# The seven activation blocks of batch 1 fetched through another engine's queue

## The chip, the cores and the metric

One core of a Trainium2 chip runs the kernel. The metric is the device time of one execution in microseconds (us). Five engines run programs of their own and meet at semaphores: TensorE (PE), VectorE (DVE), ScalarE (ACT), GpSimd (POOL) and SyncE (SP). SP computes nothing here; it issues transfers (DMAs). ACT can issue transfers as well, from its own queue, in the order of its program. The transfers of both queues are carried by the core's 16 DMA engines.

## The reference

```python
x = L0_attn_hidden_states                      # (2, 1024, 512)
x = x + layernorm(attn(layernorm(x)))          # 32 heads of 128, decaying linear attention
x = x + layernorm(ffn(layernorm(x)))           # ternary weights, FF = 1792

# attn(x):
qkv = silu(x @ qkv_w.T)                        # per head q, k, v of 128
# scan over blocks of the sequence, per head:
scores = (q @ k.T) * diag_decay
out = scores @ v + (q * q_decay) @ kv
kv = kv * block_decay + (k * k_decay).T @ v
# then
normed = norm_w * rms_normalised(out)
result = (sigmoid(x @ gate_w.T) * normed) @ out_w.T
```

## The kernel before

The attention part runs over 16 pairs of heads for batch 0 and then 16 pairs for batch 1, one window per pair and batch: windows 0 to 31 (`PAIRS` is 16, `STEPS` is 32). Window `w` projects K, Q, V and the gate G of its pair (kinds `KK, QQ, VV, GG`) and at the same time finishes the attention of window `a = w - 1`.

Each projection is one step of Strassen's scheme in Winograd's form: seven products of weight combinations with seven activation blocks, `B_11, T_2, T_3, B_21, T_1, B_22, T_4`. A product is written (kind, i); `FACTORS` gives its block: 1 uses B_11, 2 B_21, 3 B_22, 4 T_4, 5 T_1, 6 T_2, 7 T_3. Every operand is split in a high and a low float32r part, so a block in `xb` is 128 partitions x 2 x 1024 values, 8 KB a partition, 1 MB. The blocks of batch 0 are made on the chip. Those of batch 1 are made in window 0 and parked in DRAM (`x_blocks`); they have to replace batch 0's in `xb` at the passage from window 15 to window 16. Block `b` may be overwritten once the last product of window 15 that reads it, (G,i), is done; product (K,i) of window 16 waits for its arrival (`xb_in[b]`). PE's order of the G products is 1, 6, 7, 2, 5, 3, 4, and window 16's K products have the order 1, 6, 7, 2, 5, 3, 4 too.

K and V have to be turned into token order. `turn_k` transposes on DVE, and SP writes the result to DRAM and reads it back (`k_write`, `k_read`); V is written first (`v_write`), read back in four parts of 128 KB (`v_read`, `v_tok<-v_blocks`) and then transposed on DVE (`turn_v(w, s, h)`, halves s of the sequence, heads h). `v_read(w, 1)` goes into the same buffer as `v_read(w, 0)` and waits for its two transposes. The buffer then takes the output weights (`out_weights`, `v_tok<-w_out`), which wait for the transposes of the second read.

The order on each engine is the order in which its program is written. On SP, at the end of a window: `v_write` 1 and 0, `v_read` 0, the weights of V for the next window, `v_read` 1, the decay table, then the next window's G weights and the output weights. On DVE, at the end of a window: `turn_v(w,0,0)`, `finish_12` of G, `turn_v(w,0,1)`, an addition, `finish_21` of G, an addition, `turn_v(w,1,0)`, `turn_v(w,1,1)`. On ACT: the activation of V's last block (`activate(w, VV, OUT21)`), then the four sigmoids of G (`OUT11, OUT22, OUT12, OUT21`); OUT12 waits for `finish_12`, OUT21 for `finish_21`. Behind window 15, DVE reduces the largest integer weights to `part_max` (L1546), and POOL makes an all-reduce over the partitions of it (L717) ahead of its work for window 16, whose first steps are the weight sums `ws` (L530 to L538) of V. ACT's `w_hi` (L852) needs those.

In windows 2 to 15 ACT also issues three small loads `check<-w_ints` per window (L915); they are the only transfers on its queue.

## Time and profile before

| | |
|---|---|
| median of 3 runs | 2528.63 us (2528.07 to 2534.14) |
| the profiled execution's time | 2531.22 us |
| its span, first to last instruction | 2529.1 us |
| granted TensorE clock, mean | 0.976 |
| PE busy | 94% |
| POOL busy | 65% |
| DVE busy | 55% |
| ACT busy | 45% |
| SP's queue (q1) | 269.39 MB, 32.2% of the 16 engines' span |
| ACT's queue (q10) | 11.01 MB, 1.4% |
| `xb<-x_blocks`, SP | 7 transfers of 1024 KB, median 8.4 us from issue to landing |

Times within the trace are us from the start of the span. Idle time of an engine that nobody waits for costs nothing; what matters is whose wait ends last. The window of interest is the passage from window 15 to window 16, about 1060 to 1140.

### The profile page before, as it was taken

What the parts mean: (1) busy time and instruction counts of PE and PEld (TensorE: products, weight loads), DVE (VectorE), ACT (ScalarE), POOL (GpSimd) and SP (SyncE); (2) the same over time, 40 slices, a digit from 0 to 9 for tenths busy, and PEclk for the clock granted to TensorE, in tenths of its full rate; (3) what the DMA queues carried; (4) which work ended last, traced back from release to release, by engine and by line L of the source; (5) the groups of instructions that cost most, each with busy time, mean ns of one, the idle gap of its engine ahead of it and who ended that gap; (6) DMA issues with size and microseconds to landing.
All of it is one profiled execution on the core that took longest, in us unless ns stands there. A gap on an engine that the chain in (4) does not pass through costs nothing.

```text
span 2529.1 us, 38203 instructions
## 1 busy us (share of the span) xinstructions
PE 2384.8 (94%) x12256; PEld 2023.9 (80%) x12256; DVE 1396.5 (55%) x2454; ACT 1140.3 (45%) x1666; POOL 1637.1 (65%) x1311
## 2 busy tenths in 40 slices
PE   4799999999999999989999999999999996799996
PEld 3688888888888888878888888888888885577884
DVE  5456566666666666545555555555555555534347
ACT  6544444444444444434444444444444443643333
POOL 4577777777777777656777777777777763344345
PEclk8899999999999999999999999999999998899998
DMA  3633333333333333444333333333333333101001
GB/s 109 212 120 123 124 124 123 123 121 126 124 118 124 122 124 124 144 173 146 113 112 112 112 112 112 112 112 112 112 112 112 112 100 134 59 26 50 25 25 67
DMA packets 145541, 281.09 MB, mean 111 GB/s; under 512 B 20560, under 2 KB 86096, under 8 KB 143184
## 3 DMA queue, kind: packets, MB, share of 16 engines
q1 hardware_dynamic: 139440, 269.39, 32.2%
q10 hardware_dynamic: 6048, 11.01, 1.4%
q8 instruction: 30, 0.49, 0.1%
q14 instruction: 23, 0.19, 0.0%
HBM read 199.60 MB, written 80.74 MB: 111 GB/s over the span
## 4 chain that ended last, share of the span: by engine, by line
PE 55%; POOL 15%; issue 11%; DMA 7%; DVE 5%; ACT 5%; SPq 1%; POOLq 0%; ACTq 0%; DVEq 0%
PE proj L1750 33%; PE yp L1750 10%; PE sc L1816 3%; POOL qd L567 3%; PE sc L1819 3%; PE sc L1793 3%; PE sc L1806 3%; POOL sumsq L579 2%; POOL g_lo L583 2%; DMA v_tok<-v_blocks 2%; POOL h_lo L684 2%; POOL w_lo L552 2%; DMA k_blocks<-pd 2%; DMA k_tok<-k_blocks 1%; DVE stats L1196 1%
## 5 line engine op out<-in xcount | busy, mean ns | idle before, releaser
L1750 PE MATMUL proj<-xb,w_hi 128*128 128x512 f32 x3584 | 1151.8, 403 | 47.1 <-POOL w_lo L545 12.8
L1750 PEld LDWEIGHTS proj<-xb,w_hi 128*128 128x128 f32 x3584 | 653.3, 191 | 177.0 <-POOL w_lo L545 13.6
L1750 PE MATMUL proj<-xb,w_lo 128*128 128x512 f32 x1792 | 705.3, 394 | 0.0
L1750 PEld LDWEIGHTS proj<-xb,w_lo 128*128 128x128 f32 x1792 | 339.3, 189 | 74.7
L552 POOL TENSOR_TENSOR w_lo<-ws,w_hi 128x1024 fp32r<-128x1024 f32 x128 | 307.4, 2401 | 135.5 <-ACT w_hi L852 135.5
L567 POOL TENSOR_TENSOR qd<-q,table 128x512 f32<-128x512 f32 x128 | 164.6, 1298 | 202.2 <-ACT q L892 202.2
L545 POOL TENSOR_TENSOR w_lo<-raw,w_hi 128x768 fp32r<-128x768 f32 x128 | 235.6, 1841 | 15.5 <-ACT w_hi L846 15.3
L558 POOL TENSOR_TENSOR ow_lo<-v_tok,ow_hi 128x1024 fp32r<-128x1024 f32 x32 | 76.4, 2387 | 248.3 <-ACT ow_hi L860 248.3
L1385 DVE TENSOR_TENSOR g<-sc,g 128x512 f32<-128x512 f32 x128 | 88.4, 691 | 241.9 <-ACT sq L906 241.8
L1392 DVE TENSOR_TENSOR y<-yp,y 128x512 f32<-128x512 f32 x240 | 163.6, 682 | 93.7 <-PE yp L1750 93.2
L1750 PE MATMUL yp<-ow_hi,g_hi 128*128 128x512 f32 x512 | 204.8, 400 | 10.4 <-POOL g_lo L583 5.6
L1750 PE MATMUL yp<-ow_hi,g_lo 128*128 128x512 f32 x512 | 201.0, 393 | 0.0
L1750 PE MATMUL yp<-ow_lo,g_hi 128*128 128x512 f32 x512 | 201.0, 393 | 0.0
L1816 PE MATMUL sc<-pd,v 128*128 128x128 f32 x1024 | 188.7, 276 | 9.6 <-DVE state L1377 9.6
L1750 PE MATMUL proj<-x_hi,f_hi 128*128 128x512 f32 x448 | 177.2, 396 | 8.7 <-DVE x_lo L1576 8.6
L684 POOL TENSOR_TENSOR h_lo<-hid,h_hi 128x512 fp32r<-128x512 f32 x56 | 72.3, 1290 | 163.1 <-ACT h_hi L1106 163.1
L1816 PEld LDWEIGHTS sc<-pd,v 128*128 128x128 f32 x1024 | 161.1, 193 | 19.6 <-issue 9.7
L1750 PE MATMUL proj<-x_lo,f_hi 128*128 128x512 f32 x448 | 176.7, 394 | 0.0
L1819 PE MATMUL sc<-qd,state 128*128 128x128 f32 x896 | 174.3, 276 | 0.0
L583 POOL TENSOR_TENSOR g_lo<-g,g_hi 128x512 fp32r<-128x512 f32 x128 | 162.4, 1294 | 8.6 <-ACT g_hi L911 8.6
L1346 DVE STREAM_TRANSPOSE v<-v_tok 128x512 f32<-128x512 f32 x128 | 86.6, 696 | 144.9 <-DMA v_tok<-v_blocks 144.9
L579 POOL TENSOR_TENSOR sumsq<-sumsq,sq 128x512 f32<-128x512 f32 x124 | 160.9, 1298 | 4.7
(161 smaller groups left out, 4245.2 us busy)
## 6 DMA issues: line engine op xcount, KB each, us to landing
raw<-w_attn SPq DMA_DIRECT2D x128, 512.0 KB, 3.5
k_blocks<-pd SPq DMA_DIRECT2D x64, 512.0 KB, 3.5
k_tok<-k_blocks SPq DMA_DIRECT2D x256, 128.0 KB, 2.8
v_blocks<-vf SPq DMA_DIRECT2D x64, 512.0 KB, 2.7
v_tok<-v_blocks SPq DMA_DIRECT2D x256, 128.0 KB, 2.8
v_tok<-w_out SPq DMA_DIRECT2D x32, 512.0 KB, 3.6
check<-w_ints ACTq DMA_DIRECT2D x42, 256.0 KB, 3.4
table<-tables SPq DMA_DIRECT2D x32, 258.0 KB, 3.7
```

Source lines behind the costliest of these rows:

```text
L545: pool.tensor_tensor(w_lo[:, slot, A_11:A_22 + 1], raw[:, slot, A_11:A_22 + 1], w_hi[:, slot, A_11:A_22 + 1].bitcast(F32), ALU.subtract).t ...
L552: pool.tensor_tensor(w_lo[:, slot, S_1:S_4 + 1], ws[:, :, :, :], w_hi[:, slot, S_1:S_4 + 1].bitcast(F32), ALU.subtract).then_inc(wlo_s_don ...
L567: pool.tensor_tensor(qd[:, s, h].rearrange("p (c n) -> p c n", c=CH), q[:, h, half(s)].rearrange("p (c n) -> p c n", c=CH), decay.unsqueez ...
L579: pool.tensor_tensor(total, total, sq[:, h], ALU.add).then_inc(ss_done, 1)
L583: pool.tensor_tensor(g_lo[:, h], g[:, h, half(s)], g_hi[:, h].bitcast(F32), ALU.subtract).then_inc(glo_done, 1)
L684: pool.tensor_tensor(h_lo[par][:, t], hid[:, t], h_hi[par][:, t].bitcast(F32), ALU.subtract).then_inc(hlo_done, 1)
L1346: dve.transpose(v[:, s, :, h].rearrange("p c (i d) -> p c i d", i=QUADS), v_tok[:, :, h].rearrange("p i c t -> p c i t")).then_inc(v_done, 1)
L1385: dve.tensor_tensor(at, sc[h][:, :], at, ALU.mult).then_inc(gated_done, 1)
L1392: dve.tensor_tensor(y[:, t], yp[t % 2][:, :], y[:, t], ALU.add).then_inc(yacc_done, 1)
L1750: last = pe.matmul(psum, s, m, start=start and n == 0, stop=n == len(terms) - 1, skip_group_check=more)
L1816: last = pe.matmul(sc[h][:, chunk(c)], v[:, s, c, h], pd[:, s, h, c], start=True, stop=not inter)
L1819: last = pe.matmul(sc[h][:, chunk(c)], state[:, h, (c - 1) % CH], qd[:, s, h, chunk(c)], start=False, stop=True)
```

## The change

SP's program loses the seven `activations(b, i)`; ACT's gets them, in window 15 alone. Each still waits for its product (G,i) of window 15 and then issues one transfer of 1 MB. The order of the blocks stays the same, but for B_22, which is now ahead of T_4 by a sigmoid. The place of each is behind an activation that itself waits for a product at least as late. What PE waits for is as before.

```diff
             def window(w, pair, ...):          # sync
                 v_write(w, 1)
                 v_write(w, 0)
-                if second_batch:
-                    activations(B_11, 1)
                 v_read(w, 0)
-                if second_batch:
-                    activations(T_2, 6)
-                    activations(T_3, 7)
                 if next_weights:
                     weights(w + 1, VV, ...)
                 v_read(w, 1)
-                if second_batch:
-                    activations(B_21, 2)
-                    activations(T_1, 5)
                 if next_weights:
                     pair_table(w + 1, ...)
-                if second_batch:
-                    activations(B_22, 3)
-                    activations(T_4, 4)
...
+            def activations(b, i):             # scalar
+
+                act.wait_ge(proj_done, products_until(PAIRS - 1, GG, i))
+                act.dma_start(xb[:, b].bitcast(F32), x_blocks[b]).then_inc(xb_in[b], 16)
...
                 activate(w, VV, OUT21)
+                if second_batch:
+                    activations(B_11, 1)
+                    activations(T_2, 6)
                 activate(w, GG, OUT11)
+                if second_batch:
+                    activations(T_3, 7)
+                    activations(B_21, 2)
                 activate(w, GG, OUT22)
+                if second_batch:
+                    activations(T_1, 5)
                 if next_weights:
                     split_hi_s(w + 1, QQ)
                 activate(w, GG, OUT12)
+                if second_batch:
+                    activations(B_22, 3)
                 if next_weights:
                     split_hi_a(w + 1, QQ)
                 activate(w, GG, OUT21)
+                if second_batch:
+                    activations(T_4, 4)
```

On SP, from V's write in window 15 to the output weights, before:

```order
L374 DMA v_blocks<-vf 128x1024 x2
L390 DMA xb<-x_blocks 128x2048
L384 DMA v_tok<-v_blocks 32x4x256 x4
L390 DMA xb<-x_blocks 128x2048 x2
L344 DMA raw<-w_attn 128x1024
L384 DMA v_tok<-v_blocks 32x4x256 x4
L390 DMA xb<-x_blocks 128x2048 x2
L356 DMA table<-tables 128x516
L390 DMA xb<-x_blocks 128x2048 x2
L344 DMA raw<-w_attn 128x1024
L349 DMA v_tok<-w_out 128x1024
```

and now:

```order
L374 DMA v_blocks<-vf 128x1024 x2
L384 DMA v_tok<-v_blocks 32x4x256 x4
L344 DMA raw<-w_attn 128x1024
L384 DMA v_tok<-v_blocks 32x4x256 x4
L356 DMA table<-tables 128x516
L344 DMA raw<-w_attn 128x1024
L349 DMA v_tok<-w_out 128x1024
```

The seven `xb<-x_blocks` are gone from the line; V's write and its two reads follow each other with only weights between them.

On ACT, from the last activation of V in window 15 (`vf<-vf`) over the four sigmoids of the gate (`g<-...`), now:

```order
L876 ACTIVATE vf<-vf 128x4x4x32
L904 DMA xb<-x_blocks 128x2048 x2
L874 ACT_TABLE_LOAD
L874 ACTIVATE g<-proj 128x512
L904 DMA xb<-x_blocks 128x2048 x2
L874 ACTIVATE g<-g 128x512
L904 DMA xb<-x_blocks 128x2048
L836 ACTIVATE w_hi<-ws 128x1024
L874 ACTIVATE g<-g 128x512
L904 DMA xb<-x_blocks 128x2048
L830 ACTIVATE w_hi<-raw 128x768
L874 ACTIVATE g<-g 128x512
```

Before, the same activations stood there without the transfers; the last one comes right behind the fourth sigmoid.

## Rows read from the trace of the kernel before

**Rows 1.** Page: busy us, share of the span and instructions of each engine.

```profile
PE 2384.8 (94%) x12256; PEld 2023.9 (80%) x12256; DVE 1396.5 (55%) x2454; ACT 1140.3 (45%) x1666; POOL 1637.1 (65%) x1311
```

**Rows 2.** Timeline, DVE (start us, us, engine line op out<-in): once per window.

```profile
1005.57 0.43 DVE L1362 COPY b_prev<-table 128x2 f32<-128x2 f32 x1
...
1069.94 0.32 DVE L1362 COPY b_prev<-table 128x2 f32<-128x2 f32 x1
...
1149.05 0.16 DVE L1362 COPY b_prev<-table 128x2 f32<-128x2 f32 x1
```

**Rows 3.** Waits of PE, 1073 to 1142: total us, times, longest us.

```profile
PE proj L1750 <- DMA xb<-x_blocks: 4.8, 1, 4.8
PE proj L1750 <- ACT g L876: 2.8, 1, 2.8
PE proj L1750 <- DVE k L1312: 2.4, 1, 2.4
```

**Rows 4.** Timeline, PE: `contributions(15,0,0)`, then product (G,2) of window 16.

```profile
1077.52 1.05 PE L1806 MATMUL sc<-v,kd 128*128 128x128 f32 x8
...
1137.98 1.22 PE L1750 MATMUL proj<-xb,w_hi 128*128 128x512 f32 x2 [2.79 <-ACT g L876]
```

**Rows 5.** Timeline, DVE, POOL and ACT, from V's turns to the copy of g.

```profile
1073.63 0.71 DVE L1346 STREAM_TRANSPOSE v<-v_tok 128x512 f32<-128x512 f32 x1 [3.37 <-DMA v_tok<-v_blocks]
...
1082.55 1.30 DVE L1346 STREAM_TRANSPOSE v<-v_tok 128x512 f32<-128x512 f32 x2 [5.25 <-DMA v_tok<-v_blocks]
1083.78 0.11 DVE L1546 TENSOR_REDUCE part_max<-ints_max 128x1 f32<-128x3 f32 x1
...
1095.94 0.81 POOL L530 TENSOR_TENSOR ws<-raw 128x256 f32<-128x256 f32 x1 [8.86 <-issue]
...
1099.17 1.06 ACT L852 ACTIVATE w_hi<-ws 128x1024 fp32r<-128x1024 f32 x1 [1.04 <-POOL ws L538]
...
1137.33 0.60 ACT L876 ACTIVATE g<-proj 128x512 f32<-128x512 f32 x1 [10.85 <-POOL g_lo L583]
```

**Rows 6.** Windows; DMA packets of 1084:1088 and 1079.2:1081.2; `check`, issue to landing.

```profile
1065.00:1095.00 30.00, 25.19 (x121) 20.97 (x120) 13.45 (x27) 8.39 (x11) 9.76 (x9) 0.89 1.01 369
...
DMA packets 346, 1.70 MB, mean 424 GB/s; under 512 B 43, under 2 KB 43, under 8 KB 171
...
DMA packets 489, 0.52 MB, mean 258 GB/s; under 512 B 55, under 2 KB 479, under 8 KB 479
...
DMA to landing us min/median/max: 2.5/3.4/5.3
```

**Rows 7.** Timeline, SP's issues: V's write, its two reads, two blocks.

```profile
1063.61 1.57 SPq L374 DMA_DIRECT2D v_blocks<-vf  x2
...
1067.76 1.75 SPq L384 DMA_DIRECT2D v_tok<-v_blocks  x4
...
1075.60 1.75 SPq L384 DMA_DIRECT2D v_tok<-v_blocks  x4
1077.39 0.90 SPq L390 DMA_DIRECT2D xb<-x_blocks  x2
```

**Rows 8.** DMA, KB each, us to landing: passage, then window 15's start and 1003:1006.

```profile
v_blocks<-vf SPq DMA_DIRECT2D x2, 512.0 KB, 2.8
...
v_tok<-w_out SPq DMA_DIRECT2D x1, 512.0 KB, 11.3
...
v_tok<-w_out SPq DMA_DIRECT2D x1, 512.0 KB, 3.4
...
v_tok<-v_blocks SPq DMA_DIRECT2D x4, 128.0 KB, 2.8
```

**Rows 9.** Timeline, ACT: a `check` issue; V's last activation; the second sigmoid.

```profile
1051.14 0.34 ACTq L915 DMA_DIRECT2D check<-w_ints  x1
...
1064.22 0.62 ACT L892 ACTIVATE vf<-vf 128x512 f32<-128x512 f32 x1
...
1068.86 0.63 ACT L890 ACTIVATE g<-g 128x512 f32<-128x512 f32 x1 [2.11 <-DVE g L1312]
```

More of the change, by code:

```diff
@@ L385, in v_read @@
                                  v_blocks[s, :, :, b].rearrange("i d n -> d i n")).then_inc(v_in, 16)
-            def activations(b, i):
-                sp.wait_ge(proj_done, products_until(PAIRS - 1, GG, i))
-                sp.dma_start(xb[:, b].bitcast(F32), x_blocks[b]).then_inc(xb_in[b], 16)
             def stage_write(j):
@@ L399, in stage_write, with window @@
                 sp.dma_start(x_blocks[b, :, :, i], stage[:, j % 3].bitcast(F32)).then_inc(stage_out[j % 3], 16)
-            def window(w, pair, next_weights=True, second_batch=False, attn_save=False):
+            def window(w, pair, next_weights=True, attn_save=False):
                 a = w - 1
@@ L473, in _ @@
                 window(w, w)
-            window(PAIRS - 1, PAIRS - 1, second_batch=True)
+            window(PAIRS - 1, PAIRS - 1)
             window(PAIRS, 0)
@@ L915, in look_at_ints, with window @@
                 act.dma_start(check[:, :], w_blocks[c]).then_inc(check_in, 16)
-            def window(w, next_weights=True, checks=None):
+            def activations(b, i):
+                act.wait_ge(proj_done, products_until(PAIRS - 1, GG, i))
+                act.dma_start(xb[:, b].bitcast(F32), x_blocks[b]).then_inc(xb_in[b], 16)
+            def window(w, next_weights=True, checks=None, second_batch=False):
                 a = w - 1
@@ L1051, in _ @@
                 window(w, checks=3 * w - 6)
-            window(PAIRS - 1, checks=WIDTH_CHECKS - CHECKS_PER_WINDOW)
+            window(PAIRS - 1, checks=WIDTH_CHECKS - CHECKS_PER_WINDOW, second_batch=True)
             window(PAIRS)
```

## The prediction

> **What bounds the kernel now.** The page first [rows 1]: TensorE (PE) is busy 94% of the span, the next engine 65%, so in general PE decides. A change that touches one window can win or lose only what PE waits there. The copy `b_prev<-table` stands once in every window and so measures it [rows 2]: 1005.57 to 1069.94 is 64.4 us, 1069.94 to 1149.05 is 79.1 us. The passage from window 15 (batch 0's last) to window 16 (batch 1's first) costs 14.7 us more than an ordinary window. That is 0.58% of the time and the most that this change could return.
>
> Next, who PE waited for in that passage [rows 3]: 4.8 us for an activation block (`xb<-x_blocks`), 2.4 us for VectorE (DVE), 2.8 us for a ScalarE (ACT) copy of `g`. A reader who stops at the 4.8 us expects it back. The third wait is the one that ends last: PE starts product (G,2) of window 16 at 1137.98 [rows 4], whatever it did before. I follow it back [rows 5]: the copy of `g` at 1137.33 waits for GpSimd (POOL), whose chain hangs on ACT, and there `w_hi` at 1099.17 waited for POOL's `ws`. POOL's first `ws` of the window started at 1095.94, after the all-reduce of `part_max`, which DVE wrote at 1083.78, right behind `turn_v(15,1)` at 1082.55, which waited 5.25 us for `v_tok<-v_blocks`. So the end of the passage hangs on the **second read of V**, `v_read(15,1)`, and what follows takes 1137.98 - 1082.55 = 55.4 us, a fixed chain. After (G,2) everything runs on at PE's pace, so what this chain gains or loses reaches the end. The PE wait of 4.8 us lies beside it: were it gone, the third wait would grow by as much.
>
> Last, the DMA engines. From 1065 to 1095 they are busy 1.01 of the time [rows 6]; v_tok, the weights and seven blocks of 1 MB share them. What matters is in which order the bytes go, and no more can be moved.
>
> **The change, part by part.** *Removed from SP:* seven issues of about 0.43 us and their waits. SP has no other work in these stretches than the issues themselves, and the products that it waits for are early (they run in PE's program ahead of window 16, which starts before 1077.52 [rows 4]), so nearly nothing is returned here. What is returned is order: until now B_11 stood ahead of `v_read(15,0)` on SP's queue, T_2 and T_3 ahead of `v_read(15,1)`, and the other four (two of them in [rows 7]) ahead of `w_out`. That is why `w_out` took 11.3 us to land against 3.4 in an ordinary window [rows 8].
>
> *Added to ACT:* seven issues. ACT's issue of `check` took 0.34 us [rows 9], two blocks on SP 0.90 [rows 7]; beside running activations that is 0, in front of idle ones 0.45 us each. ACT idles 2.11 us in front of the second sigmoid [rows 9], which hides the first four; without that cover it would be 7 x 0.45 = 3.2 us of ACT, still not on the V chain. I take 0.
>
> *Moved:* B_11 and T_2 follow the activation of V that starts at 1064.22 [rows 9], T_3 and B_21 follow the first sigmoid (1066), T_1 the one at 1068.86. Before, B_21 and T_1 went out at 1077.39 [rows 7]. Five blocks are thus issued by 1069.3, and they travel on ACT's queue **beside** V's write and reads, no longer in a line with them. B_22 and T_4 wait for the last two sigmoids, which come behind DVE steps that stand behind `turn_v(15,0)`.
>
> **How long V takes beside them.** With blocks and little else in flight, 1.70 MB in 4 us pass at 424 GB/s [rows 6], or 26.5 GB/s for each of 16 engines. The V packets: 489 packets, 0.52 MB, in 2 us, 1 KB each, so some 30 per engine in 2 us, 0.067 us each. Of the 346 packets of the first stretch 175 are not under 8 KB; that is the size of a block's row in one partition, so the blocks go in 8 KB packets: 0.31 us each, eight per engine and block, 2.5 us a block. V's read has 4 x 128 packets, 32 per engine. How two queues share an engine, this trace hardly shows: the only ACT transfer, `check`, took 2.5 us at least and 5.3 us at most beside SP's traffic [rows 6]. So each doubles the other roughly; I take the turn to be **one packet each**, with the small one going by beside the large, 0.31 us per pair. Then:
> - `v_blocks<-vf` (issued 1063.61, landing 2.8 us after issue [rows 7, 8]): the second write has eight 4 KB packets per engine, 1.2 us alone, 2.5 beside B_11. `v_read(15,0)` goes out 1.2 us later, at 1069.0, first packets at 1070.0.
> - By then 15 of the 40 block packets of an engine have gone (from 1065.4 at 0.31). 25 are left, 7.7 us, in which 25 V packets pass; the other 7 take 0.5. End 1078.2, landed 1078.8. Before, `turn_v(15,0)` started at 1073.63 [rows 5]: **+5.2 us**.
> - DVE's steps up to the issue of `v_read(15,1)` took 1073.63 to 1075.60, so it goes out at 1080.8, packets from 1081.9. Against it stand B_22 and T_4, issued at about 1080.2 and 1082.1, with 14 packets left: 4.3 us, then 18 V packets alone, 1.2. Landed 1087.9, before 1082.55: **+5.4 us**.
> - The fixed chain of 55.4 us then puts (G,2) at 1143.3, and the profiled execution's 2531.22 us at 2536.6. It lies 2.6 above the median shown, so against 2528.63 the forecast is **2534.0**.
>
> What is next in line does not save it. The block wait of PE goes (B_21 has landed by 1076), but `contributions(15,0,0)`, which started at 1077.52 [rows 4], now waits for V until 1080.7, 3.2 us. `w_out` goes out at 1089.2 and lands 3.4 later at 1092.6, not 1095.2: a gain on DVE's scaling and `ow_hi`, but `w_hi` behind it waits for `ws` at 1104.5. PE has 2.8 us to spare in front of (G,2) and 5.4 more by the delay, so small PE stalls on the way cost nothing.
>
> The Trainium skill speaks against the purpose of such a move (DMA: Bandwidth & Descriptors, "Issuing engines are not separate DMA queues"): all issuers use the same 16 engines and interleave, and a second one saves only issue time. The 1.01 busy share agrees. By that sentence alone the time would stay at 2528.6.
>
> **Rivals.** *Longer turns, slower.* If an engine serves a run of block packets before it returns to V, or if a V packet adds its own 0.067 us to the 0.31 (0.38 a pair), then V's write lands 2.5 us late instead of 1.2, `v_read(15,0)` about 8 and `v_read(15,1)` about 9 us late: 2537.6, with ends from 2536.4 to 2540. For it: `check`'s 5.3 us; nothing in the trace excludes it. It passes the bound of 0.3% (7.6 us, about what a measurement of this kernel can tell from no change) once V is over 7.6 us late. The Trainium skill has this rule (same page, "Queues, rings and completion order"): engines go round the queues and drain a whole packet of some 9 to 17 descriptors before they switch. That would put about one block in front of each of the four parts of a read.
>
> *V is not disturbed, faster.* If SP's packets hardly wait, B_11 and T_2/T_3 no longer stand in front of them. Parts of a read landed 2.8 us after issue in an ordinary window [rows 8]: the last part of `v_read(15,0)`, out at 1069.1, would land at 1071.9 (1.7 early), and `v_read(15,1)`, out 1.7 early, at 1078.0, 4.5 early. All that follows is 4.5 earlier: 2524.1. Against it: the engines are full and V's packets are the small ones. Even this is inside 0.3%.
>
> *The late V is absorbed.* Of the 12 us from `part_max` to `ws`, POOL may spend a part on preparing the all-reduce, which would run beside the longer wait, and B_11 may start late on ACT. Then +5.4 shrinks to about 0: 2528.6. POOL's own row is rough here, so I can't exclude it.
>
> *It doesn't do what it says.* The waits on products are met before ACT comes to them, since the sigmoids in front of them wait for the same products, so the issue times are set by ACT's order, and the change does act. Small.
>
> **How the numbers follow.** Packet by packet: 0.45, of which 0.06 passes 7.6 us. Longer turns: 0.26, of which 0.23 passes. Undisturbed: 0.16, of which 0.05 passes 7.6 us the other way (if PE's waits shrink more than the chain). Absorbed or without effect: 0.13. Faster by over 0.3% 0.05, within 0.66, slower 0.29. Range: low 2524.0 is the undisturbed case, high 2539.5 nearly the far end of longer turns.
>
> **What the changed profile would show.** `xb<-x_blocks` on ACTq from 1064 on, B_21 at about 1066.5. `turn_v(15,0)` at 1079 and `turn_v(15,1)` at 1088, both waiting for `v_tok<-v_blocks`; parts of `v_tok` that land 6 us and more after their issue, against 2.8 in an ordinary window [rows 8]; `part_max` at 1089, `ws` at 1101, (G,2) at 1143; the window 84.5 us instead of 79.1. No PE wait for `xb`. If `turn_v` comes at 1072 and 1078, SP's packets aren't held and the forecast is wrong in sign. If V is late but `ws` is not, the fixed chain was not fixed.

## The result, and the profile after

The changed kernel takes 2539.22 us, median of 8 runs (2533.54 to 2542.07), against 2530.26 for the kernel before (8 runs, 2528.07 to 2534.14). The ratio is 1.003, with a 95% interval of 1.0018 to 1.0043: slower by 7.6 us, 4.6 to 10.9, by the ratio (the medians differ by 9.0). The forecast of 2534.0 was 5.4 us above its base; sign and range were right, the size came out larger, at the 0.3% that the prediction had named as about what can be told from no change. The profiled execution of after takes 2541.26 us (span 2539.2, mean granted clock 0.974), 10.0 more than the profiled one of before.

The page of after, busy times and the two queues, answers to [rows 1]:

```profile
PE 2388.1 (94%) x12256; PEld 2027.1 (80%) x12256; DVE 1394.6 (55%) x2454; ACT 1140.2 (45%) x1666; POOL 1637.5 (64%) x1311
...
q1 hardware_dynamic: 138432, 262.05, 31.0%
q10 hardware_dynamic: 7056, 18.35, 2.2%
```

No engine has more instructions, and the busy times agree within 3.3 us; 7.34 MB went over from one queue to the other. Most of the loss is idle time. The timeline of after on DVE, `b_prev` (answers to [rows 2]):

```profile
1071.35 0.31 DVE L1363 COPY b_prev<-table 128x2 f32<-128x2 f32 x1
...
1158.10 0.43 DVE L1363 COPY b_prev<-table 128x2 f32<-128x2 f32 x1
...
1227.41 0.16 DVE L1363 COPY b_prev<-table 128x2 f32<-128x2 f32 x1
```

The window of the passage takes 86.75 us instead of 79.11 (+7.6), and the next 69.31 instead of 64.52 (+4.8). All windows ahead of it together add 1.4, and what comes behind these two gives 3.8 back. How much of this belongs to this one execution is seen below, where the same kernel is profiled again.

The waits of PE in 1065 to 1155 (total us, times, longest), and PE's timeline, answer to [rows 3, 4]:

```profile
PE sc L1807 <- DVE v L1347: 7.5, 1, 7.5
PE proj L1751 <- DVE k L1299: 6.6, 1, 6.6
PE proj L1751 <- ACT g L860: 3.3, 1, 3.3
...
1086.29 2.05 PE L1807 MATMUL sc<-v,kd 128*128 128x128 f32 x8 [7.52 <-DVE v L1347]
...
1099.60 1.22 PE L1751 MATMUL proj<-xb,w_hi 128*128 128x512 f32 x2 [6.56 <-DVE k L1299]
...
1149.90 0.72 PE L1751 MATMUL proj<-xb,w_hi 128*128 128x512 f32 x2 [3.32 <-ACT g L860]
```

The wait for a block is gone. In its place PE waits for V's first turn (7.5) and for a step of K that stands behind V's second turn on DVE (6.6). The third wait, at (G,2), is still there, 10.5 us later after `b_prev` (78.55 against 68.04).

The first two waits are not harmless beside the third. Take the wait at (G,2) off its start, and PE came to it at 1146.58 in after and at 1135.19 in before, 75.2 and 65.3 us after `b_prev`: PE was 10.0 us late before it waited there, and the wait itself grew by 0.5 only. The two waits for V and K are 14.1 us, where the block and K had held PE for 7.2. The granted clock adds some: from 1100 to 1110 its mean is 0.79 in after and 1.00 in before (1.00 is 2.4 GHz, and part of the stretch in after ran at 1.2), after PE had stood idle for the 6.6 us. From these means that is an estimated 2.1 us.

DVE and POOL, answering to [rows 5]:

```profile
1084.24 0.71 DVE L1347 STREAM_TRANSPOSE v<-v_tok 128x512 f32<-128x512 f32 x1 [12.58 <-DMA v_tok<-v_blocks]
...
1097.60 1.30 DVE L1347 STREAM_TRANSPOSE v<-v_tok 128x512 f32<-128x512 f32 x2 [9.68 <-DMA v_tok<-v_blocks]
1098.83 0.11 DVE L1547 TENSOR_REDUCE part_max<-ints_max 128x1 f32<-128x3 f32 x1
1098.86 0.68 DVE L1299 TENSOR_TENSOR k<-proj,k 128x512 f32<-128x512 f32 x1
...
1099.08 0.38 POOL L701 PARTITION_ALL_REDUCE all_max<-part_max  x1 [10.25 <-DVE part_max L1547]
1107.21 0.72 POOL L514 TENSOR_TENSOR ws<-raw 128x256 f32<-128x256 f32 x1 [7.75 <-issue]
```

SP's and ACT's issues, answering to [rows 7, 9], with the activation of V behind which the first two blocks are written:

```profile
1065.01 1.57 SPq L374 DMA_DIRECT2D v_blocks<-vf  x2
1077.38 1.74 SPq L384 DMA_DIRECT2D v_tok<-v_blocks  x4
...
1062.40 0.60 ACT L860 ACTIVATE g<-proj 128x512 f32<-128x512 f32 x1 [9.85 <-POOL g_lo L567]
1062.68 0.34 ACTq L904 DMA_DIRECT2D xb<-x_blocks  x1
...
1063.06 0.44 ACTq L904 DMA_DIRECT2D xb<-x_blocks  x1
...
1064.74 0.33 ACTq L904 DMA_DIRECT2D xb<-x_blocks  x1
...
1065.11 0.46 ACTq L904 DMA_DIRECT2D xb<-x_blocks  x1
1065.62 0.62 ACT L876 ACTIVATE vf<-vf 128x512 f32<-128x512 f32 x1
```

The first block goes out 2.9 us **before** the activation starts that stands ahead of it in the program, and four are out or on their way when V's write goes. It goes 0.28 us behind the start of a copy of `g` that had waited 9.85 us for POOL. Its own product (G,1) was no reason to wait that long: E6 below, where SP waits for nothing but that product, issues the same block 16.9 us ahead of `b_prev`, and here it is 8.7.

From V's write to its first read there are 12.4 us, against 4.2 before. V's write was issued at 1065.01, and this is all that the DMA view has for 1065 to 1068 of after (packets, MB, share of the 16 engines):

```profile
q10 hardware_dynamic: 157, 1.16, 101.6%
```

Not one packet of SP's queue moved. Its first started at 1068.70, 3.7 us behind the issue; in before it was 0.8 us (1064.45).

The landings of after, 1063.5 to 1092 (KB each, median us to landing), answer to [rows 8]:

```profile
xb<-x_blocks ACTq DMA_DIRECT2D x6, 1024.0 KB, 10.0
v_blocks<-vf SPq DMA_DIRECT2D x2, 512.0 KB, 9.7
v_tok<-v_blocks SPq DMA_DIRECT2D x8, 128.0 KB, 5.4
```

Last, the view that I should have read to its end for before too, the chain of work that ended last, here of after in 1060 to 1115 (start, us, what):

```profile
1066.26 11.10 DMA v_blocks<-vf
...
1078.69 5.53 DMA v_tok<-v_blocks
...
1084.24 0.04 DVE v L1347
...
1084.88 0.66 DVE g L1320
...
1085.57 0.33 ACT g L874
...
1086.10 0.84 ACT w_hi L830
...
1087.01 1.78 POOL w_lo L529
...
1088.82 10.17 issue
...
1099.53 7.68 issue
1107.21 0.72 POOL ws L514
```

It doesn't pass through the second read of V. It goes from the **first** turn of V over `finish_12` of the gate (L1320), ACT's third sigmoid and its `w_hi`, to POOL's `w_lo`, and from there through the 18.4 us that lie between `w_lo` and `ws`, around the all-reduce. This is the road that ends at the third wait. That PE was late by itself doesn't show in it.

### The profile page after: what moved, and what is told of

It is laid out like the page before. It is cut to its first block, busy times and chain, and to the rows that moved or that the text cites. A ratio compares the mean times of both kernels' runs of the same rounds, so it can differ in the third digit from the quotient of the medians.

```text
span 2539.2 us, 38203 instructions
## 1 busy us (share of the span) xinstructions
PE 2388.1 (94%) x12256; PEld 2027.1 (80%) x12256; DVE 1394.6 (55%) x2454; ACT 1140.2 (45%) x1666; POOL 1637.5 (64%) x1311
## 4 chain that ended last, share of the span: by engine, by line
PE 59%; POOL 13%; issue 11%; DMA 7%; DVE 5%; ACT 4%; SPq 1%; POOLq 0%; ACTq 0%; DVEq 0%
PE proj L1751 36%; PE yp L1751 11%; PE sc L1817 3%; PE sc L1794 3%; PE sc L1820 3%; PE sc L1807 3%; POOL qd L551 2%; POOL h_lo L668 2%; POOL sumsq L563 2%; POOL g_lo L567 2%; DMA k_blocks<-pd 2%; POOL w_lo L536 2%; DMA v_tok<-v_blocks 1%; DMA k_tok<-k_blocks 1%; DMA v_blocks<-vf 1%
## 5 line engine op out<-in xcount | busy, mean ns | idle before, releaser
L1751 PE MATMUL proj<-xb,w_hi 128*128 128x512 f32 x3584 | 1155.3, 404 | 48.7 <-POOL w_lo L529 13.6
```

What stands on the lines that cost most here:

```text
L1751: last = pe.matmul(psum, s, m, start=start and n == 0, stop=n == len(terms) - 1, skip_group_check=more)
```

## The experiments

All but the row of after (its ratio is the one above) are compared with the kernel before on the same chip, which took 2525.8, 2525.6 and 2525.8 us there in three groups. Times in the table are us after `b_prev` of window 15; (G,2) is PE's product of window 16: "PE comes to" it at its start less its wait. "Window 17" is the `b_prev` of that window.

| kernel | ratio (95%) | first turn | second turn | first `ws` | PE comes to (G,2) | (G,2) starts | window 17 |
|---|---|---|---|---|---|---|---|
| before | | 3.7 | 12.6 | 26.0 | 65.3 | 68.0 | 143.6 |
| after | 1.003 (1.0018 to 1.0043) | 12.9 | 26.3 | 35.9 | 75.2 | 78.6 | 156.1 |
| after, again | 1.003 (1.0018 to 1.0042) | 12.7 | 25.0 | 34.8 | 73.8 | 75.1 | 149.8 |
| e1 four blocks ahead, SP | 1.0039 (1.0026 to 1.0052) | 14.0 | 21.4 | 36.4 | 75.6 | 78.9 | 153.2 |
| e2 ACT, behind V's write | 1.0031 (1.0022 to 1.0041) | 13.0 | 26.2 | 35.8 | 74.8 | 77.6 | 151.9 |
| e3 no blocks | 0.9973 (0.9963 to 0.9982) | 2.5 | 9.1 | 21.2 | 60.2 | 62.3 | 136.6 |
| e4 before, all-reduce later | 1.001 (1.0001 to 1.0019) | 4.1 | 13.2 | 10.8 | 65.1 | 66.2 | 145.7 |
| e5 after, all-reduce later | 1.0037 (1.0016 to 1.0058) | 12.8 | 25.1 | 17.4 | 71.5 | 71.5 | 150.2 |
| e6 three blocks early, SP | 1.0008 (0.9996 to 1.0019) | 2.4 | 8.7 | 26.3 | 65.1 | 67.9 | 145.9 |
| e10 e6, all-reduce behind `ws` | 1.0 (0.9991 to 1.0009) | 2.9 | 10.0 | 7.5 | 65.4 | 68.1 | 142.4 |
| e13 after, `part_max` early | 1.0031 (1.0016 to 1.0045) | 12.8 | 25.0 | 34.6 | 73.7 | 75.4 | 151.7 |
| e8 after, DVE order | 1.0 (0.9989 to 1.0011) | 17.8 | 23.8 | 22.6 | 69.1 | 69.1 | 143.9 |
| e11 before, DVE order | 0.9987 (0.9975 to 0.9999) | 5.4 | 13.1 | 21.8 | 64.9 | 66.0 | 143.8 |
| e12 all of it | 0.9976 (0.9964 to 0.9988) | 5.4 | 11.9 | 20.3 | 63.9 | 63.9 | 136.8 |

**after, again.** The changed kernel, unedited, beside other experiments.

> The changed kernel once more, beside the next three on one chip. First turn of V 12.9 us, first ws 35.9 us, (G,2) 78.6 us after b_prev of window 15, as in its first profile; time 0.3% above the kernel before.

2532.52 us against 2525.80, ratio 1.003 (1.0018 to 1.0042). The result repeats. Window 17 is 6.2 us later than before here, not 12.4, and (G,2) 7.1 us and not 10.5. The two profiled executions stand at opposite ends: 2541.26 us is near the top of the first group's runs, 2527.88 the lowest of this group's ten. A difference of 3 us between two single traces is no finding. In the profiled execution of after the granted clock fell in window 17, behind a wait of PE, which the windows view shows (stretch, its length, busy us of PE, PEld, DVE, ACT and POOL with counts, PEclk, DMA share, GB/s):

```profile
1160.00:1170.00 10.00, 8.62 (x37) 7.12 (x36) 5.03 (x9) 2.52 (x4) 7.01 (x6) 0.78 0.66 192
1170.00:1180.00 10.00, 10.00 (x48) 8.46 (x47) 5.09 (x13) 2.38 (x4) 0.00 (x0) 0.88 0.69 268
```

In the repeated one it stayed at 1.00 in 1160 to 1180. The trace of before has such a fall at (G,2) itself (0.74 in 1135 to 1140, 0.58 in 1140 to 1145), which both traces of after lack: from (G,2) to `b_prev` of window 16 before takes 11.1 us and they take 8.2. So the last column of the table carries a few us of the clock, and the steps ahead of it are the safer measure.

### What makes V late

Two reasons stood against each other: the bytes put in front of V's read, whatever queue they are on (A), or the sharing between two queues (B). E1 puts the same four blocks ahead of V's write on SP's own queue; nothing is shared.

```diff
+                if second_batch:
+                    sp.wait_ge(proj_done, products_until(PAIRS - 1, GG, 2))
+                    activations(B_11, 1)
+                    activations(T_2, 6)
+                    activations(T_3, 7)
+                    activations(B_21, 2)
                 v_write(w, 1)
                 v_write(w, 0)
-                if second_batch:
-                    activations(B_11, 1)
                 v_read(w, 0)
                 if second_batch:
-                    activations(T_2, 6)
-                    activations(T_3, 7)
+                    activations(T_1, 5)
...
                 v_read(w, 1)
-                if second_batch:
-                    activations(B_21, 2)
-                    activations(T_1, 5)
```

> The kernel before, all blocks on SP's queue, but B_11, T_2, T_3 and B_21 issued together behind product (G,2) and ahead of V's write, T_1 behind the first read of V. So the order of the bytes is about that of the changed kernel, on one queue. Theory A (4 MB stand ahead of V's write, whichever queue carries them): 4 x 2.5 us pass first, V's write lands 10 to 12 us after its issue, the first turn of V 8 us late against the kernel before, time 2536 to 2540. Theory B (the harm is that two queues share each engine): in one line V's reads are not slowed, the first turn at most 3 us late, time 2529 to 2533.

2536.44 us, +0.39%, as A expected. V's write, issued at 1062.39, landed 13.5 us later, and the first turn came at 14.0. (SP had waited for (G,2), so the write went out 1.7 us later than in before; that is part of it.) One queue in line costs the first turn as much as two side by side.

E2 keeps the change, but ACT waits until V's write has landed before it issues four blocks in a row, so that only the reads can be shared.

```diff
                 activate(w, VV, OUT21)
+                activate(w, GG, OUT11)
                 if second_batch:
+                    act.wait_ge(v_out[1], 16 * PAIRS)
+                    act.wait_ge(v_out[0], 16 * PAIRS)
                     activations(B_11, 1)
                     activations(T_2, 6)
-                activate(w, GG, OUT11)
-                if second_batch:
                     activations(T_3, 7)
                     activations(B_21, 2)
```

> The changed kernel, but ACT waits for V's write to have landed before it issues the first four blocks (behind the first sigmoid). Theory A (the blocks ahead of V's write do the harm): V's write lands 2.8 us after issue again, the first read goes out 8 us earlier than in the changed kernel, time within 2 us of the kernel before, 2528 to 2532. Theory B (sharing an engine between the queues does it): the write is fast but the first read, 32 packets of an engine each beside a block's packet at 0.31 to 0.38 us a pair, takes 10 to 12 us to land, and the second some 8; time 2537 to 2541.

V's write landed 2.6 us after its issue, as in an ordinary window, but the read went out at 1067.15 and its turn came at 1082.64, 15.5 us later, against 5.9 in before. The time is 2533.94, +0.31%, between what the two theories had said. Packets of both queues in 1074 to 1077 of e2 (packets, MB, share of the 16 engines):

```profile
q10 hardware_dynamic: 139, 1.01, 91.6%
q1 hardware_dynamic: 137, 0.12, 13.8%
```

ACT's queue carries the blocks (8 KB packets), SP's the parts of V (1 KB). Of these packets 32 are under 512 B, 16 on each queue, which leaves 123 of 8 KB and 121 of 1 KB: one for one. Equal counts over 3 us could also come from turns of eight packets each. What speaks against that is after, where SP's queue has just come in with packets of 4 KB: from 1069 to 1070 ACT's queue moved 33 packets and SP's 31, 17 to 14 in the first half and 16 to 17 in the second. A 4 KB packet takes 0.16 us there, so sixteen engines in turns of eight would have moved some 50 in the first half. The two queues take turns **packet by packet**.

A pair costs 3 x 16 / 123 = 0.39 us. That is the additive 0.38 of my rival and not the 0.31 that I took: beside the other queue an 8 KB packet itself takes 0.36 (91.6% of 3 x 16, by 123). The Trainium skill (DMA: Bandwidth & Descriptors, "Queues, rings and completion order") says that engines go round the queues by packets of some 9 to 17 descriptors; what the trace calls a packet alternates one by one here, and the measurement decides. Its going round is confirmed, and so is the price: a 1 KB packet waits for an 8 KB one.

One by one holds only once both queues are under way. Where blocks were issued on ACT's queue ahead of it, SP's first packet starts 3.1 to 3.8 us behind its issue (nine cases in the two traces of after, e2, e8 and e13), against 0.8 to 1.0 on free engines (before, e2, e3, e6). For three first reads, whose issue fell where the blocks were nearly through, it is 1.5 to 2.2. So the rival's other branch, a run of block packets before V gets a turn, is true at the entry: the extra 2.2 to 3.0 us are seven to nine packets of 0.31 us. What makes it is not shown.

E1 and E2 are each explained by their own theory, and give nearly the same delay. What they share with after is the bytes. From the issue of V's write to the last packet of its first read, 3.9 blocks pass in e1, 4.0 in e2 and 4.7 in after, against 1.1 in before, at 2.5 us a block. They lie ahead of the write, between its packets or between those of the read; the queue decides only where.

E3 leaves the seven transfers out (batch 1's products read batch 0's blocks).

```diff
                 v_write(w, 0)
-                if second_batch:
-                    activations(B_11, 1)
                 v_read(w, 0)
-                if second_batch:
-                    activations(T_2, 6)
-                    activations(T_3, 7)
...
-            window(PAIRS, x_wait=True)
+            window(PAIRS)
```

> The kernel before without the seven block transfers: batch 1's products read batch 0's blocks, so the output is not the reference's. It prices the 7 MB in the passage. Theory A (the end of the passage hangs on the second read of V, which waits in the DMA engines): first turn of V about 2 us earlier, second 5 us earlier, PE's 4.8 us wait gone, output weights 8 us earlier; (G,2) of window 16 5 us earlier or more, time 2522 to 2525. Rival (the passage is long for POOL's all-reduce and the K round trip alone): (G,2) moves less than 2 us, time 2528 or more.

2518.51 us, ratio 0.9973: all seven blocks cost the kernel before 6.8 us (4.5 to 9.3), by the ratio. With the change they cost 7.6 more, about twice as much. Even with none, (G,2) waits 2.08 us.

### Which link carries the delay

E4 (on before) and E5 (on after) take the all-reduce out of the road: POOL does it behind window 16.

```diff
             window(PAIRS - 1)
+            window(PAIRS)
             pool.wait_ge(part_done, 1)
             pool.partition_all_reduce(all_max[:, :], part_max[:, :], P,
                                       bass.bass_isa.ReduceOp.max).then_inc(all_max_done, 1)
-            window(PAIRS)
```

> The kernel before with POOL's all-reduce moved behind window 16. Theory A (chain as read: turn of V, part_max, all-reduce, ws, w_hi; the output weights' ow_hi comes only 1.0 us before ws): gain 1 us, 2529; the first ws of window 16 starts at about 1082, w_hi then waits for ow_hi. Rival (the all-reduce alone sets the passage): (G,2) up to 8 us earlier, 2522. Rival (it is off the path): no change at all in (G,2).

> The changed kernel with POOL's all-reduce moved behind window 16. In the changed kernel ow_hi ends at 1106.3 and w_hi starts 3.9 us later, at 1110.2, when ws is there. Theory (POOL's road over the all-reduce sets (G,2) of window 16): (G,2) comes 3 to 4 us earlier after b_prev of window 15 than in the changed kernel, 75 us for 78.6; the time gains 0 to 4 us, since the same move on the kernel before gained 1.9 us at (G,2) and gave it back in window 17. Rival (PE's two stalls behind V set the passage, 7.5 and 6.6 us): (G,2) does not move.

`ws` started at 10.8 in E4 and 17.4 in E5, not at 26.0 and 35.9, so the all-reduce was in the road. But `w_hi` of V came at 28.2 and 33.2, because ACT's `ow_hi`, which needs `w_out`, stands ahead of it; (G,2) gained 1.9 in E4, and its wait was gone in E5. Both gave it back in the next window, where the all-reduce stood now: E4 ended at +0.10% (1.0001 to 1.0019), E5 at +0.37% (1.0016 to 1.0058), no better than after. Moving that cost out of one window only brought it to the next.

The pair tells more. The timeline of PE in e5:

```profile
1076.68 2.05 PE L1807 MATMUL sc<-v,kd 128*128 128x128 f32 x8 [7.45 <-DVE v L1347]
...
1088.92 0.76 PE L1751 MATMUL proj<-xb,w_hi 128*128 128x512 f32 x2 [4.66 <-DVE k L1299]
...
1133.29 0.71 PE L1751 MATMUL proj<-xb,w_hi 128*128 128x512 f32 x2
```

Here POOL doesn't hold PE at (G,2) at all, and (G,2) still comes 5.3 us later than in E4 (71.5 and 66.2), window 17 4.5 us later. PE's own waits for V's first turn and for K do that: 12.1 us, where E4 has 8.3 in all. So late V reaches PE on **two roads**: straight, over the two turns, and through POOL. The first alone makes (G,2) 5.3 us late, where after has 7.1 and 10.5.

E6 does the opposite of after, on SP's queue: three blocks ahead of V's write, each as soon as its product is done, so that they are through before V comes.

```diff
-                v_write(w, 1)
-                v_write(w, 0)
                 if second_batch:
                     activations(B_11, 1)
-                v_read(w, 0)
-                if second_batch:
                     activations(T_2, 6)
                     activations(T_3, 7)
+                v_write(w, 1)
+                v_write(w, 0)
+                v_read(w, 0)
```

> The kernel before with B_11, T_2 and T_3 issued on SP ahead of V's write, each as its product of window 15 ends (about 1053, 1058 and 1060), when the DMA engines stand still. Theory (what counts is how many bytes stand between V's write and the end of its reads): 3 of 7 MB are gone from there, turn of V at the level of the kernel without blocks (2.5 and 9 us after b_prev, for 3.7 and 12.6), the block wait of PE gone or under 1 us, ws 2 to 5 us earlier, the time 3 to 6 us below the kernel before. Rival (SP, held by the waits on products, is late for V's write): first turn later than 4 us after b_prev, no gain.

A miss. Both turns came early (2.4 and 8.7), `part_max` at 10.0 instead of 13.8, and yet `ws` started at 26.3 and (G,2) at 67.9; the time was +0.08%, no gain. The timeline of POOL in E6:

```profile
1086.77 0.38 POOL L716 PARTITION_ALL_REDUCE all_max<-part_max  x1 [11.39 <-issue]
```

11.39 us of "issue" in front of the all-reduce, and `part_max` had been there for 8.5 of them, since 1078.28. In E3, with no blocks, the gap was 6.71. The same row of before, which I had not weighed:

```profile
1086.71 0.38 POOL L717 PARTITION_ALL_REDUCE all_max<-part_max  x1 [8.48 <-issue]
```

The gap began at 1078.23, right behind POOL's `w_lo`, and `part_max` (1083.78, [rows 5]) fell into the middle of it. So POOL may prepare the all-reduce from `w_lo` on, and the second read of V may never have been in POOL's road.

E10 is E6 with the all-reduce behind the first `ws`.

```diff
                 combine_weights(w, VV)
+                if reduce_max:
+                    pool.wait_ge(part_done, 1)
+                    pool.partition_all_reduce(all_max[:, :], part_max[:, :], P, ...)
                 split_out_lo(a)
...
-            pool.wait_ge(part_done, 1)
-            pool.partition_all_reduce(all_max[:, :], part_max[:, :], P, ...)
-            window(PAIRS)
+            window(PAIRS, reduce_max=True)
```

> As the three blocks early on SP, and POOL makes the all-reduce behind the weight sums ws of V of window 16 instead of ahead of them, so that w_hi of V has its input early and the 14 to 18 us of the all-reduce lie beside the wait for the output weights. Theory: w_hi waits only for ow_hi, ow_lo and w_lo come when the all-reduce ends, (G,2) 2 to 5 us earlier than with the three early blocks alone; time 6 to 10 us below the kernel before. Rival (w_lo and not w_hi is what counts, since it stands behind the all-reduce either way): no gain over the three early blocks.

`ws` started at 7.5, `w_hi` came 3.6 us earlier (25.6), and (G,2) at 68.05, as before; ratio 1.0 (0.9991 to 1.0009). A second miss: POOL's `w_lo` and what leads to the copy of `g` stand behind the all-reduce wherever it is put in that window.

The new theory for POOL's road: first turn of V, `finish_12` of G, third sigmoid, `w_hi` and `w_lo` of Q, all-reduce, `ws`. Its rival, my prediction's: second turn, `part_max`, all-reduce. E13 moves `part_max` ahead of V's turns in after, and nothing else.

```diff
                 keep_b(w)
+                if last_first:
+                    dve.wait_ge(max_done, WIDTH_CHECKS + 1)
+                    dve.tensor_reduce(part_max[:, :], ints_max[:, :], AX.X, ALU.max).then_inc(part_done, 1)
                 turn_v(w, 0, 0)
...
-            window(PAIRS - 1, checks=WIDTH_CHECKS - CHECKS_PER_WINDOW)
-            dve.wait_ge(max_done, WIDTH_CHECKS + 1)
-            dve.tensor_reduce(part_max[:, :], ints_max[:, :], AX.X, ALU.max).then_inc(part_done, 1)
+            window(PAIRS - 1, checks=WIDTH_CHECKS - CHECKS_PER_WINDOW, last_first=True)
```

> The changed kernel with part_max alone made early, ahead of the first turn of V; finish_12 and finish_21 stay behind the turns. Theory C (the first read holds finish_12, the sigmoids, w_lo of Q and so POOL's arrival at the all-reduce): little gain, 0 to 3 us at the first ws, because the all-reduce waited for part_max there 10.25 us where its preparation takes 6.7 to 11.4 us; the time stays 0.2 to 0.4% above the kernel before. Theory of the prediction (second read, part_max, fixed chain): ws some 9 us earlier, the time back at the kernel before.

2533.08, ratio 1.0031 (1.0016 to 1.0045), the same as after. The timeline of e13, DVE and POOL:

```profile
1067.41 0.14 DVE L1466 TENSOR_REDUCE part_max<-ints_max 128x1 f32<-128x3 f32 x1
...
1093.01 0.38 POOL L701 PARTITION_ALL_REDUCE all_max<-part_max  x1 [8.50 <-issue]
```

`part_max` is 27 us earlier than in after, and the all-reduce 1.9 (25.8 against 27.7 after `b_prev`). The prediction's link falls. The second read keeps a hold on PE all the same: the wait for K behind the second turn is still 4.8 us. E8 adds to E13 what the other theory names: DVE does `finish_12` and `finish_21` of G ahead of V's turns, in window 15 alone.

```diff
+                if last_first:
+                    dve.wait_ge(max_done, WIDTH_CHECKS + 1)
+                    dve.tensor_reduce(part_max[:, :], ints_max[:, :], AX.X, ALU.max).then_inc(part_done, 1)
+                    finish_12(w, GG)
+                    add_out(a, 6, first)
+                    finish_21(w, GG)
+                    add_out(a, 7, first)
+                    turn_v(w, 0, 0)
+                    turn_v(w, 0, 1)
+                else:
...
```

> The changed kernel, but in window 15 DVE makes part_max, finish_12 and finish_21 of G and the two additions ahead of the first turn of V. It cuts the link between the first read of V and POOL: the third and fourth sigmoid, w_hi and w_lo of Q no longer stand behind the turn. Theory C (POOL reaches the all-reduce late because of the first read, and then needs a fixed 14 to 18 us): POOL reaches it some 10 us earlier, ws of window 16 starts 8 to 10 us earlier, at 26 to 28 us after b_prev instead of 35.9; V's turns stay late; the time falls by 3 to 8 us below the changed kernel's, as far as PE's stalls for V let it. Theory of the prediction (the second read, part_max and what follows is the fixed chain): part_max is early here too, so both would gain; they part at the first ws: fixed after part_max, it would be 12 us behind part_max, at 14 to 15 us after b_prev, before POOL has come there with preparation. Rival (nothing but the DMA load): no gain.

2525.23, ratio 1.0 (0.9989 to 1.0011): the whole loss of the change is gone, while V's first turn is 4.9 us later still than in after. The timelines of e8, DVE, POOL and PE:

```profile
1066.65 0.69 DVE L1320 TENSOR_TENSOR g<-proj,g 128x512 f32<-128x512 f32 x1 [0.28 <-PE proj L1759]
...
1083.83 1.30 DVE L1347 STREAM_TRANSPOSE v<-v_tok 128x512 f32<-128x512 f32 x2 [12.41 <-DMA v_tok<-v_blocks]
...
1080.97 0.38 POOL L701 PARTITION_ALL_REDUCE all_max<-part_max  x1 [8.77 <-issue]
1088.58 0.72 POOL L514 TENSOR_TENSOR ws<-raw 128x256 f32<-128x256 f32 x1 [7.23 <-issue]
...
1085.28 2.05 PE L1815 MATMUL sc<-v,kd 128*128 128x128 f32 x8 [11.87 <-DVE v L1347]
```

`finish_12` no longer stands behind V's turn, `ws` starts 22.6 us after `b_prev` instead of 35.9, and (G,2) doesn't wait. So late V does most of its harm through what is queued behind it on DVE.

Which road gave how much is less clear, since the new order frees both. With the third and fourth sigmoid early, B_22 and T_4 go out at 1067.38 and 1070.10, 1.4 and 4.1 us after `b_prev` instead of 14.2 and 16.0. They make the first read later and leave the second alone: DVE waits 4.6 us for it and not 9.7. PE's wait of 11.87 us at the contributions is the longest in any of these kernels, but K's is gone with it; before has 10.0 us in its three waits. Of the 6.0 us by which (G,2) is earlier than in the repeated after, 1.3 are its own wait and 4.7 PE's pace ahead of it. PE still comes 3.8 us later than in before (69.1 and 65.3); the wait of 2.8 that before has there, and its lower clock behind it, make up for that.

E11 is the same order of DVE on before.

> The kernel before with the DVE order of the last window that removed the loss of the changed kernel (part_max, finish_12, finish_21 and the additions ahead of the first turn). Theory C: POOL comes to the all-reduce 1 to 2 us earlier here, since the first read is only 3.7 us after b_prev and product (G,4) ends about then; ws 0 to 3 us earlier, the time 0 to 3 us lower. Rival (the reorder is worth 10 us by itself, whatever V does): 10 us lower.

`ws` at 21.8, (G,2) at 66.0; 0.9987 (0.9975 to 0.9999), a small gain. PE's wait for a block is the longest left, 5.13 us, and 1.06 remain at (G,2). Against this kernel E8 still shows +0.13%, but the intervals of the two overlap, so whether something of the change's loss remains under this order is open. E12 adds to it early blocks on SP's queue and brings B_22 and T_4, which filled the DMA engines ahead of `w_out`, behind it:

```diff
                 out_weights(a, ...)
+                if last_blocks:
+                    activations(B_22, 3)
+                    activations(T_4, 4)
...
+                if second_batch:
+                    activations(B_11, 1)
+                    activations(T_2, 6)
+                    activations(T_3, 7)
                 v_write(w, 1)
                 v_write(w, 0)
                 if second_batch:
-                    activations(B_11, 1)
+                    activations(B_21, 2)
                 v_read(w, 0)
                 if second_batch:
-                    activations(T_2, 6)
-                    activations(T_3, 7)
+                    activations(T_1, 5)
...
                 v_read(w, 1)
-                if second_batch:
-                    activations(B_21, 2)
-                    activations(T_1, 5)
...
-                if second_batch:
-                    activations(B_22, 3)
-                    activations(T_4, 4)
```

> The kernel before with the DVE order of e11; on SP B_11, T_2 and T_3 early, B_21 behind V's write, T_1 behind the first read, B_22 and T_4 behind the output weights. Theory: the passage at the level of the kernel without blocks or 1 to 3 us above: (G,2) 63 to 66 us after b_prev for 68.0, output weights 3 to 5 us earlier, time 3 to 7 us below the kernel before. Rival (B_22 and T_4 come too late for PE): PE waits for xb 2 us or more at (K,3), and the gain is under 3 us.

2519.94 against 2525.80, ratio 0.9976 (0.9964 to 0.9988): the best of those that keep the result, 6 us under before and, on the same chip, 12.6 under after. One wait of over 2 us is left to PE in its passage, for a block, as the rival had said, though the gain is larger than it allowed. From the timeline of e12:

```profile
1088.15 1.19 PE L1758 MATMUL proj<-xb,w_hi 128*128 128x512 f32 x2 [5.13 <-DMA xb<-x_blocks]
```

## Why the prediction was right, and where its steps failed

**The sign** was right for the right first half: blocks beside V make V late, and what PE saves on the block wait (4.8 us) it loses again on V. No block wait is left in after; the forecast of that holds.

**ACT's place** failed. I put the first four blocks behind the starts of the activations written ahead of them (1064.22 and 1066 in before). In after the first went out at 1062.68, 2.9 us ahead of such a start. An issue of ACT doesn't wait for the activations in front to run; what held it was the wait of one of them that was not yet met.

**V's write**, sized at +1.2 us, took +8.2 (4.2 to 12.4 us from its issue to that of the read). Its first packet started 2.9 us later behind its issue than in before, and then its packets took 7.8 us beside 268 of the blocks', where before has 2.6. I had counted only the second of its two transfers, and only B_11 beside it. **The first read** was sized at 9.8 us from its issue to the turn and took 6.9, since most of the block bytes had gone by then. Together the first turn came 9.2 us later, not 5.2.

**The price of a pair**, 0.31, was 0.39 in e2. One packet each was right once both queues were under way, and wrong at the entry, where a run of blocks passes first. The rival of longer turns was nearer in the price (0.38), in V's delays (2.5, 8 and 9 us) and in its total (2537.6, 9.0 above its base, as the medians have it).

**The second read** was sized at 7.1 us and took 11.4 (1086.22 to 1097.60). That makes the second turn +13.6, not +5.4. Two blocks of ACT, issued at 1085.57 and 1087.36, went beside it. Its first packet started at 1089.31, 3.1 us behind the issue where I had put 1.1, and its last at 1097.0, 7.7 us later where I had put 5.5. Nine block packets an engine at 0.39, and 23 of V alone at 0.067, explain 5.1 of these 7.7; the rest wasn't told apart.

**The fixed chain** was the step that failed in kind. I took the 12 us from `part_max` to `ws` as work that follows `part_max`. Rows 5 show `[8.86 <-issue]` on `ws`, and the all-reduce's own row has `[8.48 <-issue]`: neither waits for DVE. POOL's road was first turn, `finish_12`, sigmoid, `w_lo` (e13 and e8), so the delay that counts on it is the first turn's, +9.2, and it reached `ws` as +9.9 and (G,2) as +10.5. In the profiled after, `part_max` did come last by a little: the all-reduce waited for it and was 1.9 us later than in e13. The rival "late V is absorbed" had hold of a true thing, POOL's preparation beside the wait: of the second turn's +13.6 it took 3.7.

**PE's own stalls** failed too. I forecast 3.2 us at the contributions and called small stalls on the way free, as PE had 2.8 us to spare. It waited 7.5 us there and 6.6 for K behind the second turn, a wait that the forecast doesn't have, and came 10.0 us late to (G,2) by itself. E5 shows this road by itself: (G,2) 5.3 us later than in e4, without any wait for POOL.

**The size** then agreed within 2.2 us (5.4 and 7.6) although its term was +5.4 on a link that carried next to nothing, and the true delays, 9 to 10 us, came on two other roads side by side. That is luck: a good total is no evidence for its parts.

**No gain from a second queue.** In 1065 to 1068 of after, ACT's queue alone moved 1.16 MB, 385 GB/s with the engines full, no more than SP's had (424 in [rows 6]). The Trainium skill says that (DMA: Bandwidth & Descriptors, "Issuing engines are not separate DMA queues"), and the trace agrees; but what it concludes, that only issue time changes, left out the order of the bytes, which made 0.3% here.

Open: why the preparation of the all-reduce takes 6.0 us in e12 and 11.4 in e6. The load of the DMA engines alone doesn't set it: it was 6.7 with no blocks (e3) and 10.8 to 11.4 with the engines full (e1, e6, e10), but 6.6 in e11, where they were full too (share 1.05). Open as well: how the loss divides between the two roads. No kernel freed PE's turns of V and left POOL's road late.

## What to carry to other kernels

When a transfer moves to another queue, ask which small, awaited transfers its bytes will now lie beside, from what moment on, and what is queued behind the engine that waits for them; the length of the wait that the move removes says little. Follow the chain of waits in the view that gives it through every link, and take an idle gap put down to "issue" as work of the engine itself that its last semaphore may have nothing to do with. Before a stall is called free because a later wait has slack, take each wait from the start of its instruction and see when the engine came there. And look at the order on the waiting engine: here the steps of DVE that don't need V, put ahead of its turns, brought the changed kernel back to the time of before.

## What the runs showed of the hardware

- A DMA issue in ACT's program doesn't wait for the activations ahead of it to run: it went out 2.9 us before one of them started (1062.68 against 1065.62). It did stand behind a wait that was not met: 0.28 us behind the start of the copy that had waited 9.85 us for POOL. To place a transfer behind an activation takes a wait on something that the activation makes.
- Two queues under way alternate packet by packet, whatever the packets' sizes (123 of 8 KB to 121 of 1 KB in e2, 33 of 8 KB to 31 of 4 KB in after), so 1 KB packets beside 8 KB ones pass at 0.39 us each.
- A queue that comes in while another fills the engines waits longer for its first packet: 3.1 to 3.8 us behind the issue in nine cases (3.7 for V's write in after), against 0.8 to 1.0 on free engines.
- The partition all-reduce keeps POOL from other work for 14.0 to 19.2 us in this place (e12, e6), from the step ahead of it to the first `ws` behind it, although its own row shows 0.38: 6.0 to 11.4 ahead of it, 6.6 to 8.9 behind.
